# POOL waits for all stores of the output, behind its last one, at the end of a graph-attention and mixture-of-experts kernel

## The reference

```
x = x + gnn(layernorm(x), adj, W, a)
    # Wh = h @ W; e = leaky_relu(s1[i] + s2[j]); softmax over the row's edges; attn @ Wh
x = x + ffn(layernorm(x), gate_w, gate_b, W1, b1, W2, b2)
    # probs = softmax(xf @ gate_w + gate_b); the two largest of 8 experts for each token
    # out = sum over these two of prob * (gelu(xf @ w1 + b1) @ w2 + b2)
```

## Time and profile before

| | us |
|---|---|
| median of 3 runs (lowest, highest) | 362.03 (361.08, 362.18) |
| the profiled execution | 361.37 |
| its span, from the first to the last instruction | 359.5 |
| outside the span | 1.87 |
| mean granted TensorE clock | 0.919 |

### The profile page before, as it was taken

One profiled execution on the slowest core, in us unless ns is written; L12 is line 12 of the kernel. 1 busy time (PEld: TensorE's weight loads), 2 busy tenths in 40 slices (PEclk: granted clock), 3 DMA queues, 4 the chain that ended last, 5 costly groups with the idle time before them and its releaser, 6 DMA issues.

```text
span 359.5 us, 9425 instructions
## 1 busy us (share of the span) xinstructions
PE 310.7 (86%) x2390; PEld 280.3 (78%) x2390; DVE 244.4 (68%) x1056; ACT 249.4 (69%) x796; POOL 178.8 (50%) x203
## 2 busy tenths in 40 slices
PE   6878598988898608599999999999999999999960
PEld 3667387777677404399899999999999999999960
DVE  5664979999988996657755666656665666566630
ACT  3568477766765411388788888888888888888830
POOL 4939200266466677757634544454444444444450
PEclk9989878898878976789999999999999999999995
DMA  6990321429911111432222212222222112121000
GB/s 190 284 292 13 111 70 50 124 61 206 131 54 38 47 54 53 104 77 86 78 66 58 63 47 54 67 60 67 69 61 70 48 53 64 49 51 50 4 0 0
DMA packets 42231, 28.07 MB, mean 78 GB/s; under 512 B 5188, under 2 KB 40030, under 8 KB 42182
## 3 DMA queue, kind: packets, MB, share of 16 engines
q1 hardware_dynamic: 37222, 18.69, 22.2%
q0 software_dynamic: 4960, 8.80, 8.2%
HBM read 16.78 MB, written 12.23 MB: 81 GB/s over the span
## 4 chain that ended last, share of the span: by engine, by line
PE 60%; DVE 24%; ACT 5%; issue 4%; POOL 3%; DMA 1%; POOLq 0%; DVEq 0%; ACTq 0%
PE at_ps L1385 24%; PE wh_ps L1364 23%; DVE rows L637 4%; PE at_ps L1383 3%; PE q_ps L1354 3%; PE at_ps L1292 2%; ACT probs L442 2%; DVE bn L657 2%; DVE less_max L615 2%; DVE lrelu L610 2%; PE q_ps L1284 2%; DVE bn L665 1%; DMA xin<-in_x 1%; PE wh_ps L1251 1%; POOL rstd_start L299 1%
## 5 line engine op out<-in xcount | busy, mean ns | idle before, releaser
L348 POOL DMA_INDIRECT out_x<-o_sb,xt x91 | 89.7, 986 | 98.7 <-DVE o_sb L1173 91.6
L548 ACT ACTIVATE hid<-wh_ps,pair_w 128x128 f32<-128x128 f32 x364 | 104.1, 368 | 24.1 <-PE wh_ps L1364 23.9
L1385 PE MATMUL at_ps<-experts,hid 128*128 x728 | 110.8, 287 | 0.0
L1364 PE MATMUL wh_ps<-xnT,pair_w 128*128 128x128 f32 x728 | 98.3, 279 | 0.1
L1385 PEld LDWEIGHTS at_ps<-experts,hid 128*128 128x128 f32 x728 | 96.1, 192 | 2.2
L341 POOL DMA_INDIRECT sorted_rows<-rows,pos x64 | 62.5, 976 | 60.9 <-DVE pos L838 43.5
L1364 PEld LDWEIGHTS wh_ps<-xnT,pair_w 128*128 128x128 f32 x728 | 90.2, 195 | 0.6 <-issue 0.4
L846 DVE COPY pair_w<-experts 128x258 f32 x182 | 55.0, 302 | 29.2 <-issue 20.4
L1170 DVE SCALAR_TENSOR_TENSOR o_sb<-at_ps,xt 128x128 f32<-128x128 f32 x91 | 31.9, 350 | 45.9 <-PE at_ps L1385 45.5
L557 ACT ACTIVATE xn<-xt 128x128 f32<-128x128 f32 x91 | 43.9, 484 | 0.1
L1383 PE MATMUL at_ps<-experts,ones_bf 65*128 x182 | 40.9, 225 | 0.2 <-ACT hid L548 0.2
(11 more groups left out here) (200 smaller groups left out, 391.4 us busy)
## 6 DMA issues: line engine op xcount, KB each, us to landing
xt<-sorted_rows SPq DMA_DIRECT2D x91, 66.5 KB, 1.9
xin<-in_x SPq DMA_DIRECT2D x8, 512.0 KB, 5.4
adj_sb<-in_adj SPq DMA_DIRECT2D x8, 512.0 KB, 5.3
sorted_rows<-no_row SPq DMA_DIRECT2D x1, 1862.0 KB, 19.9
out_x<-o_sb,xt POOLq DMA_INDIRECT x91
experts<-in_L_ffn_W SPq DMA_DIRECT2D x1, 1024.0 KB, 9.3
experts<-in_L_ffn_W SPq DMA_DIRECT2D x2, 512.0 KB, 8.7
sorted_rows<-rows,pos POOLq DMA_INDIRECT x64, 2.5
```

The source lines that it names most:

```text
L348: nc.gpsimd.indirect_dma_start(out=out_v, out_offset=bass.IndirectOffsetOnAxis(ap=xt[:, n % XR, TOK:TOK + 1].bitcast(I32), axis=0), in_=o_ ...
L548: last = nc.scalar.activation(hid[:, n % WR, q, :], wh_ps[:, n % WR, q * P:(q + 1) * P], ACT.Gelu, bias=pair_w[:, n % WR, k, B1 + c:B1 + c ...
L1364: last = nc.tensor.matmul(wh_ps[:, n % WR, q * P:(q + 1) * P], pair_w[:, n % WR, k, c * P:(c + 1) * P], xnT[:, n % 2, :], start=True, stop ...
L1385: last = nc.tensor.matmul(at_ps[:, n % 2, cols], hid[:, n % WR, k * HC + c, :], experts[:, bass.ds(e, 1), W2C + c * P:W2C + (c + 1) * P], ...
```

## The change

Behind its last store, POOL waits for the twelve semaphores of the stores, at the same values as SP does.

```diff
                 store_tile(n)
                 if last + 2 + n < N_GRAPHS:
                     sort_rows(last + 2 + n, last + 3 + n)
+            for k in range(XR):
+                pool.wait_ge(o_stored[k], 16 * len(range(k, NT, XR)))
```

## The result

The changed kernel takes 363.46 us (median of 22 runs, 362.23 to 366.25), the kernel before 361.36 us in the 22 runs beside it (360.83 to 363.19). The ratio is 1.0059, with an interval of 1.0044 to 1.0074: the change makes the kernel 2.1 us slower (1.6 to 2.7).

A forecast was written before the change was run, and what follows sets the result against it. POOL's DRAIN at the block's end was taken to set the end: starting at 352.1 plus 8.82 us of work, it ends at 360.92, 1.67 us later. Forecast 363.4 us, between 363.0 and 363.7; range 360.8 to 365.2.

The forecast's parts named there:

- The bound: At the block's end: POOL's DRAIN alone, 10.027 us long and ending at 359.25, sets the kernel's end.
- First term: When POOL's last DRAIN starts behind the added waits: 352.1, with bounds of 351.6 and 352.6.
- Second term: At the block's end: 8.82 us of POOL's DRAIN is work still to do after the waits; bounds 0.171 and 10.027 us.
- the larger loss: Rival: the DRAIN's work ran beside the last issue, so all 10.027 us follow the waits; 2.88 us slower, chance 0.15.
- The guess behind it: In POOL's last DRAIN: a step for each of 155 indirect DMAs issued, 0.057 us each.
- The sum: The DRAIN ends at 360.92 instead of 359.25, 1.67 us later, with nothing to hide it; forecast 363.4 us.
- The fast one: Rival: POOL's last DRAIN is short once all stores have landed; 6.98 us gained, 354.4 us, chance 0.20.
- The no-change one: Rival: POOL's DRAIN waits for the last landing, then works 7.65 us; 361.9 us, at most 0.5 us lost, chance 0.21.

The follow-up runs named there:

- e8: The kernel before, its block opened with no_gpsimd_drain=True so that POOL executes no DRAIN at the end: 354.98 us, ratio 0.9823.
- e10: The changed kernel measured again, beside the kernel before on one chip: 364.72 us, ratio 1.0088.
- e3: The changed kernel with one wait on POOL, for the last store's semaphore, instead of twelve: 363.04 us, ratio 1.0032 to the kernel before.
- e1: The changed kernel with one more DRAIN on POOL ahead of the store of tile 77: 355.68 us, ratio 0.9813.
- e4: The kernel before, without the waits on POOL, with one more DRAIN on POOL ahead of the store of tile 77: 354.91 us, ratio 0.9807.
- e5: The changed kernel with one more DRAIN on POOL behind the first 32 of its 155 indirect DMAs: 362.98 us (one execution).
- e9: The changed kernel, its first 48 indirect DMAs raising two semaphores in turn instead of one: last DRAIN 8.90 us; no whole time given.
- e6: The changed kernel with 20 small DMAs (one row of 64 bytes each) ahead of POOL's first one: 363.57 us (one execution).

## Why the prediction was right

**The bound.** Right: POOL's DRAIN sets the end in both kernels, and taking it away from the kernel before (e8) gives 6.8 us back. One reading was off, without effect on the sum: 346.28 is the end of a piece of the chain and not that of PE's last matmul. The timeline of the kernel before has it at 347.22 + 0.66 = 347.88:

```profile
347.22 0.66 PE L1385 MATMUL at_ps<-experts,hid 128*128 x4
```

In the changed kernel it ended at 347.49, and POOL's last issue at 350.04. Both are 0.39 us earlier, within the half microsecond that the prediction allowed.

**First term, the DRAIN's start.** Forecast 352.1, which is 1.67 us behind the last issue's end; measured 1.8 us in the changed kernel's trace and again in e10. POOL goes through the waits a little slower than SP (43 ns against 28 for most of them) and starts the DRAIN 0.2 us behind its branch, SP 0.1 us behind its own. The landing with one wait and the branch is 1.3 us of the term, as e3 shows, and eleven of the twelve waits are 0.5.

**Second term, the DRAIN's work.** Forecast 8.82 us, measured 8.816. The reading from ACT's and DVE's DRAINs, that its duration is the wait for the engine plus something of its own, was right, and the larger loss (10.0 us) is out with it. The guess behind it was right in kind and wrong in size: the work is for each DMA, but at 0.082 us for 107 of them, not 0.057 us for 155. That changes nothing here, since neither number depends on the waits.

**The sum.** On its own execution the forecast was 1.67 us more; the traces give 1.8, and the 22 runs of each 2.1 (1.6 to 2.7). That 363.4 us fell so near to 363.46 is in part luck: the forecast started between 361.37 and 362.03, and the 22 runs of the kernel before have their median at 361.36. A base that was 0.4 us too high made up for a loss that was 0.4 too low. Of this 0.4, the later start of the DRAIN is some 0.2, and some 0.2 seem to lie outside the span, for which the sum had no term.

**The rivals.** The fast one (a DRAIN behind landed stores is short) is refuted by the 8.816 us; a DRAIN is short when few DMAs lie behind it (1.20 us in e1). With it falls the time that follows from the rule in the Trainium skill, "PSUM — Partial Sum Buffer", section "Engine vs sequencer instructions", alone: the profile shows no instruction of POOL behind 350.04, and the DRAIN still took 8.8 us. The rule itself (a drain waits for its engine to be idle) is not refuted by this, as the rows don't show what POOL did in these 8.8 us. The no-change one (the work follows the last landing) wanted 7.2 to 7.7 us and is out as well, for the kernel as it is; e4 suggests that the DRAIN does wait for a landing, but beside its work.

## What to carry to other kernels

A wait is only free if what stands behind it needs what it waits for. Here the last instruction of the slowest engine could do its 8.8 us of work beside the landing of the last stores, and the wait put the two one after the other. Where a kernel issues many DMAs from POOL (64 and 91 here), read the DRAIN's row at the block's end, and subtract the wait for the engine: a second DRAIN in time that POOL has to spare (e1, e4) takes most of it off the end.

## What the runs showed of the hardware

- POOL's DRAIN took 0.082 us for each DMA that POOL had issued since its last DRAIN and not yet retired, and 0.06 us beside (14, 46 and 51 DMAs: 1.200, 3.813 and 4.229 us; 109 DMAs: 9.0 us). 20 of the 51 were of 64 bytes, the others of 128 rows. It took the same with the last store in flight (8.82 us) as with all stores landed (8.816 us).
- The DRAINs of ACT, PE and DVE ended within 0.1 us of their engines' last instruction (346.4 behind 346.33, 347.9 behind 347.88, 348.7 behind 348.65 in the kernel before). SP's took 7 ns, though SP had issued all loads.
- POOL stalled some 1.2 us ahead of its 114th DMA of 128 rows since the last DRAIN, in all runs that got so far but e5, where the stall was 0.5 us. By the length of the DRAINs behind it, 48 of its DMAs were retired by then (16 in e5, 47 in e9). In e6, with 20 small DMAs ahead, the first stall (0.5 us) came ahead of DMA 129 and not of 114, and the one of over 1 us ahead of DMA 134.
- Where its work was shorter than the last landing, the DRAIN ended 0.6 to 0.7 us behind SP's first wait for the stores (e4, one trace), which reads as a wait for the landing.
